# A graph layer and a mixture of experts on one core: the row's own term as a one on the adjacency's diagonal

## The reference, cut to what matters

```python
deg = jnp.maximum((adj != 0).astype(jnp.float32).sum(-1), 1.0)
y      = _layernorm(x)
a_hat  = adj + jnp.eye(4096)                 # the row's own term
dinv   = rsqrt(deg)[:, None]
pooled = (dinv * a_hat * dinv) @ y + y       # dinv is a column: row i is divided by deg[i]
x = x + relu(pooled @ W + b)
# then on layernorm(x): router, softmax, the best 2 of 16 experts,
# each expert gelu(t @ W1 + b1) @ W2 + b2, weighted sum, residuals
x = x + (t + sum_of_the_two_weighted_experts)
```

## Time and profile before

| | us |
|---|---|
| median of three runs | 668.12 |
| profiled execution | 667.72 |
| its span, first to last instruction | 666.1 |
| TensorE busy | 598.5 (90%) |
| VectorE busy | 456.1 (68%) |
| GpSimd busy | 335.6 (50%) |
| ScalarE busy | 231.9 (35%) |

### The profile page before, as it was taken

The page is one execution under the profiler, slowest core; times in us unless marked ns, Lnnn a source line. Parts: engine busy times, 40 slices in busy tenths (PEclk is TensorE's granted clock), DMA queues, the critical chain, the costliest instruction groups (busy, mean ns, idle before and its releaser), DMA issues. The chain is left out here.

```text
span 666.1 us, 17021 instructions
## 1 busy us (share of the span) xinstructions
PE 598.5 (90%) x4796; PEld 462.3 (69%) x4797; DVE 456.1 (68%) x1369; ACT 231.9 (35%) x483; POOL 335.6 (50%) x375
## 2 busy tenths in 40 slices
PE   2999999999999999999943999899999999999993
PEld 1687888888888788888831666566666777676772
DVE  2665888888888788888873666577665565565562
ACT  2785333332333222333330444343433323332331
POOL 6232466667666667766451123455444444434443
PEclk9999999999999999999975999999999999999998
DMA  8908699999999989999287344566654443343420
GB/s 228 236 13 160 132 195 196 196 193 190 190 196 180 196 171 190 193 198 200 87 316 242 99 113 110 127 141 138 136 84 75 80 80 67 67 75 64 74 49 1
DMA packets 67450, 94.60 MB, mean 142 GB/s; under 512 B 9232, under 2 KB 42288, under 8 KB 66896
## 3 DMA queue, kind: packets, MB, share of 16 engines
q0 software_dynamic: 32928, 51.03, 45.4%
q1 hardware_dynamic: 32176, 40.32, 19.7%
q10 hardware_dynamic: 2304, 2.72, 1.2%
HBM read 103.71 MB, written 25.83 MB: 194 GB/s over the span
## 5 line engine op out<-in xcount | busy, mean ns | idle before, releaser
L484 PE MATMUL bank<-wall,at_xg 128*128 128x257 f16 x1024 | 238.6, 274 | 5.9 <-DVE at_xg L832 5.8
L486 PE MATMUL bank<-wall,at_xg 128*128 128x256 f16 x1024 | 233.1, 273 | 0.0
L1299 POOL DMA_INDIRECT out_dram<-orows,at_xg x79 | 128.1, 1622 | 179.2 <-DMA out_dram<-orows,at_xg 98.0
L590 PE MATMUL bank<-wall,feat 128*128 (+1 forms) x474 | 117.2, 384 | 10.9 <-issue 7.9
L484 PEld LDWEIGHTS bank<-wall,at_xg 128*128 128x128 f16 x1024 | 102.8, 100 | 28.0 <-DVE at_xg L832 13.9
L769 ACT ACTIVATE hgs<-hgs 128x512 f32<-128x512 f32 x79 | 49.8, 630 | 198.2 <-DVE hgs L1123 195.9
L1129 DVE SCALAR_TENSOR_TENSOR hl<-bank,xseT 128x512 f16<-128x512 f32 x79 | 54.6, 692 | 92.1 <-ACT xseT L775 68.5
L1269 POOL DMA_INDIRECT rows<-feat,posi x64 | 66.7, 1042 | 91.1 <-issue 91.1
L486 PEld LDWEIGHTS bank<-wall,at_xg 128*128 128x128 f16 x1024 | 100.3, 98 | 15.0
L613 PE MATMUL bank<-wall,xseT 128*128 (+1 forms) x632 | 108.1, 273 | 0.0
L590 PEld LDWEIGHTS bank<-wall,feat 128*128 128x128 f16 x474 | 45.9, 98 | 59.1 <-issue 23.8
(11 more groups left out here) (146 smaller groups left out, 802.2 us busy)
## 6 DMA issues: line engine op xcount, KB each, us to landing
abuf<-in_adj_dram POOLq DMA_DIRECT2D x128, 256.0 KB
wst<-in_L_ffn_W_dram SPq DMA_DIRECT2D x32, 512.0 KB
at_xg<-rows SPq DMA_DIRECT2D x79, 136.0 KB
out_dram<-orows SPq DMA_DIRECT2D x32, 128.0 KB
abuf<-in_L_ffn_b_dram SPq DMA_DIRECT2D x4, 1024.0 KB
wall<-in_x_dram SPq DMA_DIRECT2D x12, 256.0 KB, 13.9
rows<-pad ACTq DMA_DIRECT2D x12, 136.0 KB, 2.7
out_dram<-orows,at_xg POOLq DMA_INDIRECT x79
```

What stands on the lines that cost most here:

```text
L484: both = [lambda: pe.matmul(ps_acc[odd][:, 0:D + 1], w, yh[:, j, 0:D + 1], start=j == 0, stop=j == T - 1), lambda: pe.matmul(ps_acc[odd][: ...
L486: lambda: pe.matmul(ps_acc[odd][:, 0:D], w, yl[:, j, :], start=False, stop=False)]
L590: mm = pe.matmul(q_h[r % 2][:, :], a, w, start=n == 0, stop=n == 3 * DC - 1)
L1299: L.indirect_dma_start(out, bass.IndirectOffsetOnAxis(ap=info[r][:, 0:1].bitcast(U32), axis=0), orow[r], None, bounds_check=N - 1, oob_is_ ...
```

## The change

`own_rows` and its two products a tile go. VectorE adds to the tile's 128 x 128 diagonal block, in the buffer in which it has arrived and before it is transposed, a constant that holds the identity in the layout of that buffer. In that layout partition group b (32 partitions) and position a of the row groups meet only where a = b, and a partition holds every second column, hence the stretch of 66 columns from which 64 are read, from column 1 for an even tile and from column 0 for an odd one. The constant `own_col` is made by GpSimd at the start. The ones of `yh` become SY, and the degree is recovered from a sum that now counts the diagonal twice.

```diff
+    own_col = sb("own_col", [P, Q, 2 * PQ + 2], F16)
...
-        def own_rows(t, odd):
-
-            for part in own_parts(t):
-                pe.matmul(ps_acc[odd][:, 0:D], id16[:, :], part, start=False, stop=False)
-
...
                     if j == JC:
-                        own_rows(0, 0)
...
                 if g == 0 and has_t:
-                    own_rows(t, odd)
                     own_product(t)
...
-        V.memset(yh[:, :, D:D + 2], 1.0).then_inc(ev("ones_made"), 1)
+        V.memset(yh[:, :, D:D + 2], SY).then_inc(ev("ones_made"), 1)
+
+        def add_own(i, k):
+
+            V.wait_ge(a_in[k % AB], (tile(i, k) - k % AB) * (16 * Q // AB) + 16 * Q)
+            if isinstance(tile(i, k), int) and tile(i, k) == 0:
+                after(V, "own_col", Q)
+            own = arrived[:, k % AB, :, :].rearrange("p a (n q) -> p n a q", q=2 * PQ)[:, bass.ds(pair(i, k), 1), :, :]\
+                .rearrange("p n a q -> p (n a) q")
+            first = 1 - k % 2
+            V.tensor_tensor(own, own, own_col[:, :, first:first + 2 * PQ], ALU.add).then_inc(ev("own_added"), 1)
 
         def transpose_chunk(i, k, c):
 
             n = tile(i, k) * CH + c
-            V.wait_ge(a_in[k % AB], (tile(i, k) - k % AB) * (16 * Q // AB) + 16 * Q)
+            after(V, "own_added", tile(i, k))
...
                 if c == 0 and k == 3:
+                    add_own(0, 0)
                     transpose_chunk(0, 0, 0)
...
-            V.tensor_scalar(deg[:, 0:1], ps_acc[odd][:, D:D + 1], 1.0, SY, ALU.max, ALU.mult).then_inc(ev("degree"), 1)
+            V.tensor_scalar(deg[:, 0:1], ps_acc[odd][:, D:D + 1], 2.0 * SY, -SY, ALU.max, ALU.add).then_inc(ev("degree"), 1)
...
                 if is_(tile(i, k2), lambda t2: 1 <= t2 < T):
+                    if c2 == 0:
+                        add_own(i, k2)
                     transpose_chunk(i, k2, c2)
...
         L.tensor_copy(id16[:, :], id32[:, :]).then_inc(ev("constants"), 1)
+        L.memset(own_col[:, :, :], 0.0).then_inc(ev("own_col"), 1)
+        for b in range(Q):
+            after(L, "own_col", b)
+            L.affine_select(out=own_col[b * PQ:(b + 1) * PQ, b, :], in_=own_col[b * PQ:(b + 1) * PQ, b, :],
+                            compare_op=ALU.not_equal, fill=1.0, base=-1, pattern=[[1, 2 * PQ + 2]], channel_multiplier=-2)\
+             .then_inc(ev("own_col"), 1)
+        after(L, "own_col", Q)
         L.wait_ge(ev("p_ones16"), 1)
```

## The result

The changed kernel takes 675.66 us (median of 6 runs, 674.92 to 676.87); beside it the kernel before takes 668.89 us (666.71 to 670.16). The ratio is 1.0103, 95% interval 1.0088 to 1.0118: the change costs 1%, 6.8 us. Forecast were 673.4 us and a range of 667.6 to 679.

A forecast was written before the change was run, and what follows sets the result against it. The prediction took a closed ring of GpSimd and VectorE, not TensorE, to bound the graph. Start 0.65, scatter delays 5.1 and end - 0.46 gave + 5.3 us: 673.0 profiled, 673.4 us median, 0.8% slower; range 667.6 to 679.

The forecast's parts named there:

- What bounds the kernel: In the graph, GpSimd and VectorE waiting for each other set 8.98 us a tile; TensorE needs only 8.3.
- the ring: Closed loop of GpSimd and VectorE waits over 26 tiles of the graph, 8.98 us each, with TensorE outside it.
- The collision: In odd steps the addition shifts the 128x1024 VectorE instruction across the second scatter's start, delaying that scatter by 0.39 us.
- Its size: Delay of the second scatter in 13 odd steps: 13 x 0.39 = 5.1 us, bounds 1.8 and 8.7.
- the length of the addition: VectorE's addition per tile: 0.42 us, 0.46 with its wait, bounds 0.21 and 0.74.
- The start: Before the 26 tiles: two delays of 0.46 us by the addition, 0.22 given back in tile 1; taken as + 0.65.
- The end: Last three tiles of the graph: TensorE gains 0.66 us, of which 0.46 reaches the table and the experts.
- the free tiles: Tiles where TensorE's period is its own 8.3 us, so the removed products save 0.22 us each.
- These do not change: The table and the experts, behind the graph, were claimed to take as long as before.
- A: Rival: the 128x1024 instruction does not hold the second scatter up; + 0.2 us, 668.3 us, no change; chance 0.24.
- B: Rival: TensorE is the bound, so 0.22 us counts in all 31 tiles; 662.2 or 661.3 us; chance 0.06.
- C: Rival: the addition itself delays the scatter by up to 0.42 us in all 26 steps; 684 us; chance 0.10.

The follow-up runs named there:

- experiment 3: The kernel before without the two identity products and with nothing in their place; 666.11 us, ratio 0.9975.
- experiment 7: The kernel before with GpSimd's four adjacency loads moved behind its power and low part, ahead of the scatters; 650.85 us, ratio 0.9749.
- (1): The changed kernel with the addition moved ahead of the transpose of chunk 2, into VectorE's idle time; 671.93 us, ratio 1.0046.
- (4): The changed kernel with the 128x1024 instruction reading a PSUM bank in place of the staged weights; 672.60 us, ratio 1.0058.
- experiment 8: The changed kernel with GpSimd's four adjacency loads moved behind its power and low part, ahead of the scatters; 653.55 us, ratio 0.9782.

## Why the prediction was right, and where its sizes were off

*What bounds the kernel.* Right. Without the products and with nothing added the period stays at 8.99 (experiment 3), and with GpSimd's loads out of the ring it falls to 8.33 (experiment 7). The 90% of TensorE were a share of its time, not a claim on the critical path.

*The collision.* Right as a mechanism, shown from both sides: shift the 128x1024 instruction back (1) or take its second SBUF input away (4), and the second scatter is at 0.99 us again and 3.1 to 3.7 us are back. The Trainium skill (SBUF — State Buffer, Who interferes with whom) says that a VectorE instruction with two SBUF inputs contends with a GpSimd instruction that reads SBUF, and infers that descriptor generation does not suffer. The scatter, which takes its places (posi) from SBUF, behaves like a GpSimd instruction that reads SBUF, and what the prediction drew from that rule, a wait only while the places are read, is too mild. The inference holds for a direct load here: in experiment 8 one that started at 218.52, with L910 running from 218.51 to 219.74, took 0.55 us. Whether it holds for the descriptors of the scatter no run shows, as none parts the reading of the places from them.

*Its size.* The term was 13 x 0.39 = 5.1 us and measured 3.5. What failed is the length of the addition: 0.42 us were taken from L1059, whose output is float32, and 0.25 to 0.30 were measured. With its wait it moves the transposes by 0.32 us in the written-out steps and by 0.42 to 0.44 in the hardware loop, where 0.13 us pass between its end and the transpose. L910, though, starts only 0.36 us later against the scatters, and as it is 0.05 us shorter in this place it ends 0.31 us later and not 0.46: 0.27 us a step and not 0.39. The additions of the even tiles, whose second operand starts at an odd element, take 0.29 to 0.30 us in the ring and those of the odd tiles 0.28 to 0.29. The whole 0.13 us between them that the prediction had from the Trainium skill (VectorE: DVE Perf Modes, Mode 2x_1P) is not there, so its rule on alignment is not borne out for that operand.

*The start.* Forecast + 0.65 us, measured + 0.32 at tile 3. The two delays by the addition are shorter than forecast (0.33 and 0.32 us, not 0.46 each), but the power's 0.34 comes on top, at the end of what I allowed: GpSimd's constants took 1.89 us more rather than 1.3. The step that failed is what the removed products give back: I counted them in tile 1 alone, and they count in the tiles 1, 2 and 3, 0.66 us instead of 0.22.

*The end.* TensorE's 0.21 us in the free tiles gave 0.43 us up to tile 31 and 0.42 us up to the last power, as forecast (0.46). None of it reaches the experts, because the next stretch is 0.8 us longer.

*What the sum did not have.* "These do not change" is the step that failed most: behind the last power 3.7 us were added, 0.8 up to the first block of tokens and 2.9 in the experts, half of the 7.2 us between the two profiled executions. Their cause stays open. The ring's term was 1.5 us too large and the start's 0.3, so the errors cancelled in part, and that the forecast came within 2.3 us of the measured time is luck as much as the mechanism's merit.

*Rivals.* A falls with 4, B with 3. C falls with the 1.03 us between L979 and L1283 in the changed kernel, where the addition runs in that interval.

## What to carry to other kernels

Before an instruction is taken from the busiest engine, look whether that engine's period is its own: a stretch of the same trace in which a neighbour has less to do shows it. Where two engines wait for each other in a ring, only the ring's own instructions count; one reordering there gave 17 us, and the products' removal 1.7. And an instruction that moves others along brings their collisions with it, so where the long two-input instructions will stand belongs to the price of a short one.

## What the runs showed of the hardware that I had not expected

A scatter that starts while VectorE's 128x1024 instruction reads two SBUF tensors ends 0.83 to 0.88 us after that instruction (0.94 for one scatter each in experiments 7 and 8), but not sooner than its own 0.99 allows: where L905 ended 0.08 us after the scatter's start, the scatter took 0.99. With PSUM in place of one of the two it is not delayed at all. Nor is one that has started first: in the earlier trace rows the first scatter starts at 195.28, L905 at 195.51, and the scatter takes 1.08 us as in a step without L905 (186.41).

The transfers were no limit at a DMA share of 0.94: with GpSimd's loads out of the ring they run faster. The windows of 100 to 300 us, of the kernel before and of experiment 7 (columns as above):

```profile
100.00:300.00 200.00, 193.08 (x1713) 161.35 (x1711) 165.52 (x628) 60.49 (x144) 135.38 (x180) 1.00 0.94 191
```

```profile
100.00:300.00 200.00, 200.00 (x1852) 177.32 (x1850) 180.63 (x686) 68.38 (x157) 151.17 (x193) 1.00 1.03 206
```

A half-precision addition of 256 elements with both inputs in SBUF takes 0.25 to 0.31 us, with an odd element offset on one of them too.
